# Who scales the last two blocks of a chunk: VectorE in odd chunks, ScalarE in even ones, in the smoothing stage of a four-layer graph network

## What is computed

```python
n = x.shape[0]
src, dst, w = _gcn_norm(edge_index, edge_weight, n)
gamma = 1.0 / (2.0 * (1.0 - LAMBDA_AMP))
hh = x
for _ in range(K):                       # K = 3
    lx = x - _spmm(x, src, dst, w, n)
    y = x - gamma * 2.0 * (1.0 - LAMBDA_AMP) * lx
    x = hh + _proximal_l21(y - hh, gamma * LAMBDA_AMP)
```

## Time and profile before

| | us |
|---|---|
| median of 3 runs | 7871.04 |
| lowest and highest run | 7860.16, 7871.34 |
| the profiled execution, its own time | 7866.05 |
| its span | 7864.0 |
| busy in the span: TensorE matmul | 6913.7 (88%) |
| busy: TensorE weight load | 5904.4 (75%) |
| busy: VectorE | 5856.1 (74%) |
| busy: ScalarE | 4368.6 (56%) |
| busy: GpSimd | 2859.4 (36%) |

### The profile page before, as it was taken

How to read it: one execution, slowest core, us unless ns; L and a number is a source line. 1 busy time by engine, 2 the same in 40 slices (tenths; PEclk the granted TensorE clock), 3 DMA queues, 4 the chain that set the end, 5 groups by cost and what they waited for, 6 DMA issues and landing times. The chain is left out here.

```text
span 7864.0 us, 279159 instructions
## 1 busy us (share of the span) xinstructions
PE 6913.7 (88%) x98724; PEld 5904.4 (75%) x98724; DVE 5856.1 (74%) x17150; ACT 4368.6 (56%) x13164; POOL 2859.4 (36%) x2959
## 2 busy tenths in 40 slices
PE   2699999999999799999995699898895999998888
PEld 1455555555555499999995698898895999997878
DVE  4466666666666589899896699899898767775556
ACT  0122222222222199999995588787795666665545
POOL 0488888888888745455453000000000000000000
PEclk9999999999999999999997899999998999998879
DMA  9522222222222267677674888888895677774645
GB/s 388 170 60 60 60 60 60 60 60 59 59 60 59 56 222 232 228 229 234 223 233 144 276 321 307 294 322 297 310 343 190 198 202 203 201 198 121 186 134 158
DMA packets 654014, 1430.31 MB, mean 182 GB/s; under 512 B 282485, under 2 KB 349812, under 8 KB 649777
## 3 DMA queue, kind: packets, MB, share of 16 engines
q1 hardware_dynamic: 540674, 1232.57, 48.7%
q0 software_dynamic: 98560, 94.35, 5.7%
q10 hardware_dynamic: 14232, 96.26, 3.2%
HBM read 987.75 MB, written 436.48 MB: 181 GB/s over the span
## 5 line engine op out<-in xcount | busy, mean ns | idle before, releaser
L340 POOL DMA_INDIRECT sorted_rows<-sort_rows,sort_row_at x1600 | 1974.9, 1234 | 579.5 <-issue 543.5
L1626 ACT ACTIVATE smooth_msg<-smooth_ps_a,smooth_w_rows 128x64 f32<-128x64 f32 x6000 | 1312.9, 333 | 269.7 <-PE smooth_ps_a L1716 254.3
L371 ACT ACTIVATE sort_count<-sort_ps_c 50x50 bf16<-50x50 f32 x1600 | 331.7, 207 | 1903.3 <-PE sort_ps_c L403 1903.3
L1401 ACT ACTIVATE poly_cast<-poly_mat 128x1536 bf16<-128x1536 uint8 x500 | 714.6, 1475 | 439.3 <-PE poly_ps L1422 365.2
L399 PEld LDWEIGHTS sort_ps_r<-sort_count,sort_hot_dt 50*125 50x125 bf16 x1600 | 283.3, 177 | 837.6 <-issue 582.7
L413 PE MATMUL sort_ps_m<-sort_w,sort_hidden 128*125 128x64 f32 x3200 | 879.3, 430 | 0.0
L1738 PE MATMUL smooth_ps_s<-smooth_msg,smooth_hot 128*128 128x64 bf16 x7500 | 775.3, 195 | 68.1 <-DVE smooth_last_part L1866 47.4
L392 PE MATMUL sort_ps_h<-sort_attrs,sort_w 24*128 24x500 f32 x800 | 812.6, 1117 | 19.1 <-DMA sort_attrs<-in_attr_t 19.1
L1738 PE MATMUL smooth_ps_s<-smooth_rest,smooth_hot 128*128 128x64 bf16 x7500 | 770.9, 194 | 15.4 <-issue 15.4
L1738 PE MATMUL smooth_ps_s<-smooth_last_part,smooth_hot 128*128 128x64 bf16 x7500 | 770.2, 194 | 9.5 <-issue 9.5
L413 PEld LDWEIGHTS sort_ps_m<-sort_w,sort_hidden 128*125 128x125 f32 x3200 | 732.1, 320 | 41.1
(11 more groups left out here) (340 smaller groups left out, 16373.8 us busy)
## 6 DMA issues: line engine op xcount, KB each, us to landing
poly_mat<-counts_t SPq DMA_DIRECT2D x500, 400.0 KB, 3.7
smooth_src<-src_rows SPq DMA_DIRECT2D x150, 960.0 KB, 5.1
smooth_hot<-hot_rows SPq DMA_DIRECT2D x150, 960.0 KB, 7.1
smooth_src<-src_rows SPq DMA_DIRECT2D x150, 640.0 KB, 6.1
smooth_hot<-hot_rows SPq DMA_DIRECT2D x150, 640.0 KB, 7.2
graph_edges<-sorted_rows SPq DMA_DIRECT2D x125, 700.0 KB
hot_rows<-graph_hot SPq DMA_DIRECT2D x125, 640.0 KB, 3.5
src_rows<-graph_hot_t SPq DMA_DIRECT2D x125, 640.0 KB, 3.4
```

The source lines that it names most:

```text
L340: pool.indirect_dma_start(out=sorted_rows, out_offset=bass.IndirectOffsetOnAxis(row_at[u][:, j:j + 1], 0), in_=rows[u][:, j, :], in_offset ...
L1401: act.activation(cast[u][h][:, DVE_S:HR, :], mat[u][h][:, DVE_S:HR, :], ACT.Copy)\
L1626: last = act.activation(at[:, i, :], ps_a[g % 2][:, i * D:(i + 1) * D], ACT.Copy, scale=w_rows[u][:, c * CHUNK + i:c * CHUNK + i + 1])
```

## The change

In chunks with odd g nothing moves. In chunks with even g (0, 2, 4, 6, 8) ScalarE scales the two blocks of `ps_v` as well, with two more ACTIVATEs behind its eight and a wait for that look-up ahead of them, and VectorE's TENSOR_TENSOR is left out. `scaled_a` is then raised after the tenth block. The waits are counted anew: `by_dve` gives the number of VectorE's scalings up to a chunk.

```diff
+        by_dve = lambda k, p, g: N_CHUNKS * p + (N_CHUNKS * k * PAIRS + (g + 1) // 2)
...
                     for i in range(BY_ACT):
                         last = act.activation(at[:, i, :], ps_a[g % 2][:, i * D:(i + 1) * D], ACT.Copy,
                                               scale=w_rows[u][:, c * CHUNK + i:c * CHUNK + i + 1])
+                    if g % 2 == 0:
+                        act.wait_ge(looked_v, number + 1)
+                        for i in range(BY_ACT, CHUNK):
+                            last = act.activation(at[:, i, :], ps_v[0][:, (i - BY_ACT) * D:(i - BY_ACT + 1) * D], ACT.Copy,
+                                                  scale=w_rows[u][:, c * CHUNK + i:c * CHUNK + i + 1])
                     last.then_inc(scaled_a, 1)
...
                         act.wait_ge(scaled_a, done)
-                        act.wait_ge(scaled_v, done)
+                        act.wait_ge(scaled_v, by_dve(k, p, -6 if u == 0 else -1))
...
-                            pe.wait_ge(scaled, number - 1)
+                            if ps is ps_a:
+                                pe.wait_ge(scaled_a, number - 1)
+                            elif g % 2 == 1:
+                                pe.wait_ge(scaled_v, by_dve(k, p, g - 2))
...
                 def scale(k, p, u, c):
+                    if (N_CHUNKS * u + c) % 2 == 0:
+                        return
                     number = N_CHUNKS * row_of(k, p, u) + c
                     dve.wait_ge(looked_v, number + 1)
-                    if c == 0:
+                    if c < 2:
                         dve.wait_ge(w_kept, row_of(k, p, u) + 1)
...
                             dve.wait_ge(scaled_a, number + 1)
-                            dve.wait_ge(scaled_v, number + 1)
+                            if (N_CHUNKS * u + c) % 2 == 1:
+                                dve.wait_ge(scaled_v, by_dve(k, p, N_CHUNKS * u + c))
                             dve.tensor_tensor(rest[c][:], msg[c][:], high(msg[c]), ALU.subtract).then_inc(firsts, 1)
```

More of the change, by code:

```diff
@@ L1708, in look_up @@
                         pe.wait_ge(src_in[u][part_of(c * CHUNK)[0]], 16 * PAIRS * k + 16 * p + 16)
-                    for ps, first, end, scaled, looked in ((ps_a, 0, BY_ACT, scaled_a, looked_a),
-                                                           (ps_v, BY_ACT, CHUNK, scaled_v, looked_v)):
+                    for ps, first, end, looked in ((ps_a, 0, BY_ACT, looked_a), (ps_v, BY_ACT, CHUNK, looked_v)):
                         if not (isinstance(number, int) and number < 2):
-                            pe.wait_ge(scaled, number - 1)
+                            if ps is ps_a:
+                                pe.wait_ge(scaled_a, number - 1)
+                            elif g % 2 == 1:
+                                pe.wait_ge(scaled_v, by_dve(k, p, g - 2))
                         for i in range(first, end):
@@ L1858, in pair @@
                                 scale(k, p, u + (c + 1) // N_CHUNKS, (c + 1) % N_CHUNKS)
[L1859 to L1863, removed]
                             beside.go(at_once)
@@ L1873, in pair @@
                     by_row[1].end()
-                scale(0, 0, 0, 0)
                 for k in range(PASSES):
@@ L1882, in _ @@
                             spilled.on_vector(dve, k, n)
-                            scale(k, p + 1, 0, 0)
                     dve.wait_ge(spilled.y_in, 16 * k + 16)
```

## The result

| | before | after |
|---|---|---|
| median of 20 runs each, us | 7871.41 | 7859.71 |
| lowest and highest, us | 7860.16, 7884.11 | 7849.97, 7872.26 |
| the profiled execution, its own time, us | 7866.05 | 7863.09 |

The ratio is 0.9985, with a 95% interval of 0.9978 to 0.9992: faster by 12 us, where 32 were forecast. The time lies inside the range of 7822 to 7872; of the gain itself less than half came.

A forecast was written before the change was run, and what follows sets the result against it. VectorE was taken to set the pair in all passes, with ScalarE next in the last after the change. Terms of -28.5, -7, +4 and 0 gave -31.5 us, so 7839 us against the median, range 7822 to 7872.

The forecast's parts named there:

- What it adds: ScalarE's ten extra ACTIVATEs a pair: 2.0 us, 17.3 to 19.3; the met wait taken as 0, register instructions beside busy engines.
- VectorE's saving: Five scalings a pair leave VectorE: 0.89 us saved in the first two passes' loop, 0.78 in the last and pairs 22 to 24.
- Direct neighbours: last_part directly behind rest on VectorE where no small step stands between: 0.85 us start to start, saving 0.09, not 0.20.
- The loop of the first two passes: 32 loop pairs, VectorE's demand going from 20.36 to 19.47 us a pair: -28.5 us.
- Pairs 22 to 24: The nine pairs 22 to 24, 24.37 us each, VectorE saving 0.78 a pair: -7 us.
- The last pass: 18 loop pairs where the bound passes from VectorE to ScalarE, 19.3 against 19.08 us: +4 us.
- The sum: All terms together -31.5 us: 7834.5 against the profiled execution, 7839 us against the median.
- Pairs 0 to 3: The first pairs of each pass: 0 change, with some +15 us over the three passes as the upper end.
- Rival (a): ScalarE's uneven chunks and hand-over to TensorE eat the gain: +25 us in 50 loop pairs, 7864; chance 0.2.
- Rival (b): ScalarE becomes the bound outright, its two extra blocks costing more than 0.20 us each: 7902 or 7906; chance 0.06.
- Rival (c): DMA becomes the bound, its share 0.90 at 19.47 us a pair, with nearly no gain: 7868; chance 0.02.

The follow-up runs named there:

- waits ahead: The changed kernel with the waits for the next chunk's scaling issued ahead of the small step: 7827.91 us, ratio 0.9951 to the kernel before.
- the kernel before with its waits ahead: The kernel before with its waits for the next chunk's scaling put ahead of the small step: 7860.31 us against 7862.75, ratio 0.9998.
- VectorE's part alone: The changed kernel without ScalarE's two extra blocks per even chunk except in the very first pair: 7831.29 us, beside 7864.86 before.
- ScalarE alone: The kernel before, with ScalarE also scaling two blocks of ps_a into a spare tile in even chunks, VectorE keeping all its work: 7875.47 us.
- a share for each pass: The changed kernel with waits ahead, ScalarE taking over in the last pass only in chunks 2, 6 and 8: 7811.32 us, ratio 0.9934.

## Why the prediction was wrong

- **The step that failed** is one sentence of "What it adds": "Register instructions that count the waits anew stay beside busy engines." They were costed at nothing, with the engine's own work as the cover, and the prediction did not ask where that cover is missing. It is missing behind each wait for a small step, where the sequencer stands still until VectorE is empty. There a register instruction is worth 0.09 us, five times a pair, so that VectorE's demand is 19.98 and not 19.47: 0.45 x 32 = 14 us of the missing gain in the first two passes, shown by taking it out (waits ahead, 19.54) and by putting it into the kernel before (20.82). Some 0.05 us a pair stay open. The front part's own rows of the order showed `L1868 REGISTER_ALU` ahead of a rest that had none before.
- **VectorE's saving** was right otherwise. With the register instructions out of the way (waits ahead) a pair is 19.54 or less. Direct neighbours are 0.85 apart. The Trainium skill's "VectorE: DVE Perf Modes", section "The DRAIN you can't avoid", says that a semaphore between chained operations costs nothing extra. The trace does not agree: last_part, which waits for rest, starts 0.85 behind it in the kernel after (4707.43 to 4708.28), while the next rest, which has no wait on last_part, starts 0.73 behind it.
- **The loop of the first two passes**: 32 x (19.98 - 20.36) = -12 instead of -28.5. The prediction counts 16 loop pairs here (327 / 20.36) and 18 in the last pass, though the loop has 18 in each. With 36 the forecast term is -32 and the measured one -14, so this is a small slip beside the 0.5 a pair.
- **Pairs 22 to 24**: 24.37 to 23.43 in the first pass, -0.94; in the last pass two roots go from 21.65 (5944.68 to 5966.33) to 20.80 (5943.46 to 5964.26), -0.85. Nine pairs give about -8 instead of -7. These are unrolled on VectorE, so that their counts are constants, and no register instruction stands behind a wait: the gap from a `smooth_shrink` step to rest is 0.035 before and after. The trace also shows where most of the 0.16 over 0.78 comes from. Behind the third step of a set and behind its last, VectorE's sequencer has a semaphore instruction that tells another engine (L1803, L1832), and in the kernel before a second one (L1855) that waits for the scaling. In even chunks VectorE scales no longer, and the second one is gone:

```profile
4881.92 0.29 DVE L1830 TENSOR_TENSOR sums_rest<-smooth_left,sums_rest 125x128 bf16<-125x128 f32 x1
4882.44 0.83 DVE L1856 TENSOR_TENSOR smooth_rest<-smooth_msg 128x640 f32<-128x640 f32 x1 [0.23 <-DVE sums_rest L1830]
...
4887.62 0.29 DVE L1840 TENSOR_TENSOR sums_rest<-smooth_left,sums_rest 125x128 bf16<-125x128 f32 x1
4888.06 0.83 DVE L1869 TENSOR_TENSOR smooth_rest<-smooth_msg 128x640 f32<-128x640 f32 x1
```

  The gap falls from 0.23 to 0.15, twice a pair in the first two passes and once in the last, whose sets end earlier. So it is not register instructions alone: a semaphore instruction of 0.021 us behind a wait costs 0.08 too. It is also where the 24.15 of the kernel before with its waits ahead comes from: there the second one stands ahead of most of these steps, and the gap is 0.15 behind all 18 of the third steps.
- **The last pass** turned over to ScalarE as forecast: 19.36 against 19.3, 18 x 0.28 = +5 instead of +4. VectorE's demand there was too low by the same step (18.63 measured alone, not 18.30), which stayed hidden behind ScalarE. The view of waits has TensorE behind ScalarE there, from 5650 to 5900 us:

```profile
PEld smooth_ps_a L1726 <- ACT smooth_msg L1634: 14.2, 52, 0.5
PE smooth_ps_a L1726 <- ACT smooth_msg L1634: 5.1, 13, 0.4
```

- **The sum** with the measured terms is -12 - 8 + 5 = -15. The matmuls of the stage's adding-up start from 4356.7 to 5996.9 us before and from 4359.9 to 5984.0 after, 16 us less. The medians differ by 12, the two profiled executions by only 3: the rest of the program, which nothing touched, was 3 us longer ahead of the stage and 10 us longer behind it in this one execution. Over the nine traces it takes 4346 to 4360 us ahead and 1860 to 1877 behind. So the last 4 us between sum and medians are not assigned.
- **Pairs 0 to 3** were costed at 0, and no change can be told. From the stage's first matmul into `ps_s` to the first root it is 124.9 us before and 124.3 after; the other seven traces have 123.5 to 127.9. At the two turns from one pass to the next the roots are 117.3 and 114.7 apart before, 115.6 and 118.3 after.
- **Rival (a)** named 7864, close to what came; that is luck, for the mechanism is another. Even its sign appeared, roots 20 apart and ScalarE idle for `ps_a`: in the first pass's loop of the kernel after, 0.58 us a pair:

```profile
ACT smooth_msg L1629 <- PE smooth_ps_a L1726: 5.8, 10, 0.6
```

  but with the waits ahead the same view of the same 200 us has

```profile
ACT smooth_msg L1629 <- PE smooth_ps_a L1726: 0.6, 4, 0.2
```

  so that wait followed from VectorE's length and was not its cause, and VectorE's part alone has roots 20.0 apart without any of ScalarE's new work. **Rival (b)** had its price at 0.27 or more for two blocks over the 0.4; ScalarE alone gives (19.45 - 19.3) / 5 = 0.03. **Rival (c)**: the DMA share is 0.88 in the first pass's loop, and 0.94 in the fastest loop measured (a share for each pass), which is faster than any other, so it does not bound these.

## What to carry to other kernels

When an instruction is taken out or moved, look at what its neighbours got from it: a count in a register, or one wait that could stand for two. In this kernel a register instruction is free while its engine computes and costs about 0.09 us on VectorE behind a wait that empties it, and a semaphore instruction there costs 0.08; where the order of instructions shows a new one directly behind such a wait, count it, and try to issue it ahead of the wait. And share out work stage by stage: the same move that gains where VectorE is the bound loses where ScalarE comes next.

## What the hardware showed that was not expected

A register instruction of 0.040 us lengthens the gap from 0.035 to 0.123, by twice its own duration, and one of 0.053 us to 0.139. A semaphore instruction of 0.021 us takes a gap from 0.15 to 0.23. So the cost of an instruction on the sequencer, where nothing covers it, is not its duration in the trace.

ScalarE's rows change their look when it has no idle time. In the kernel after, last pass, eight blocks read 1.75 us after a pause and up to 2.37 later on, though the starts stay 0.2 apart:

```profile
5706.12 2.37 ACT L1629 ACTIVATE smooth_msg<-smooth_ps_a,smooth_w_rows 128x64 f32<-128x64 f32 x8
5707.69 0.93 ACT L1657 ACTIVATE smooth_w_rows<-w_all 128x50 f32 x1
5708.90 1.75 ACT L1629 ACTIVATE smooth_msg<-smooth_ps_a,smooth_w_rows 128x64 f32<-128x64 f32 x8 [0.28 <-PE smooth_ps_s L1748]
```

From 5706.12 to 5707.69 is 1.57 for the eight. Here the durations do not tell what a block costs; the distance of starts does.
